# Attention kernel: row maxima moved inside the SBUF and turned once a pair, the scaling of the maxima on GpSimd, logarithms first among the loads

## The reference, cut to what matters

```python
log_G = cumsum(log_sigmoid(6.906768 + gate))
s = einsum('bthd,bshd->bhts', q, k) * scale
logits = 2 * log(abs(s) + 1e-30) + log_G[:, :, :, None] - log_G[:, :, None, :]
logits = where(tril, logits, -inf)
m = max(logits, axis=-1)
a = where(tril, exp(logits - m), 0)
y = einsum('bhts,bshd->bthd', a, v) / (sum(a, -1) + 1e-6)
y = (y - mean(y)) / sqrt(var(y) + 1e-9) * ln_w
```

## Time and profile before

| what | us |
|---|---|
| median of three runs | 2074.45 |
| the profiled execution's own time | 2080.6 |
| its span, first to last instruction | 2078.2 |
| TensorE busy in the span | 1939.0 |
| VectorE busy | 1765.1 |
| ScalarE busy | 1298.9 |
| GpSimd busy | 783.3 |

### The profile page before, as it was taken

The page is one execution under the profiler, slowest core; times in us unless marked ns, Lnnn a source line. Parts: engine busy times, 40 slices in busy tenths (PEclk is TensorE's granted clock), DMA queues, the critical chain, the costliest instruction groups (busy, mean ns, idle before and its releaser), DMA issues. The chain is left out here.

```text
span 2078.2 us, 37745 instructions
## 1 busy us (share of the span) xinstructions
PE 1939.0 (93%) x13187; PEld 1378.2 (66%) x13187; DVE 1765.1 (85%) x2747; ACT 1298.9 (62%) x2204; POOL 783.3 (38%) x687
## 2 busy tenths in 40 slices
PE   7999769999999999999999998799937999999997
PEld 5766525555555555555555554699837999999997
DVE  6999849999999999999999999677766878778774
ACT  5444457777777777777777775344425656656653
POOL 3777601121111112211211111366623665656553
PEclk9999979999999999999999999799966999999999
DMA  5888792455433455433555321444442433444343
GB/s 190 279 280 282 245 254 64 118 127 132 96 87 102 118 127 128 104 83 90 132 127 127 86 63 35 113 129 133 127 155 72 91 72 81 91 91 86 70 103 61
DMA packets 158247, 257.16 MB, mean 124 GB/s; under 512 B 48751, under 2 KB 122880, under 8 KB 151616
## 3 DMA queue, kind: packets, MB, share of 16 engines
q1 hardware_dynamic: 131824, 216.17, 37.3%
q0 software_dynamic: 15360, 20.99, 6.6%
q10 hardware_dynamic: 10896, 17.83, 2.6%
HBM read 159.19 MB, written 100.27 MB: 125 GB/s over the span
## 5 line engine op out<-in xcount | busy, mean ns | idle before, releaser
L999 ACT ACTIVATE att_sb_a<-att_ps_s,att_sb_fg,att_sb_f 128x1024 f32<-128x1024 f32 x384 | 454.1, 1201 | 230.0 <-PE att_ps_s L1144 218.9
L1037 DVE TENSOR_TENSOR keep_sb_store<-keep_sb_store,att_sb_a 128x1024 f32<-128x1024 f32 (+2 forms) x528 | 535.3, 1028 | 15.9 <-ACT att_sb_a L999 7.5
L955 POOL TENSOR_SCALAR_AFFINE_SELECT att_sb_dec<-att_sb_dec 128x128 f32<-128x128 f32 x256 | 178.4, 698 | 844.7 <-ACT att_sb_dec L989 844.7
L1163 PE MATMUL att_ps_off<-att_sb_a,att_sb_v 128*64 128x512 f32 x1520 | 365.5, 594 | 1.2 <-DVE att_sb_part L1064 1.1
L1855 ACT ACTIVATE ffn_sb_h<-ffn_ps_p,ffn_sb_b_cols 128x256 f32<-128x256 f32 x320 | 151.7, 476 | 179.8 <-PE ffn_ps_p L2038 152.7
L1144 PEld LDWEIGHTS att_ps_s<-att_sb_q,att_sb_k 64*128 64x128 f32 x1896 | 158.4, 185 | 115.7 <-issue 64.9
L1144 PE MATMUL att_ps_s<-att_sb_q,att_sb_k 64*128 64x512 f32 (+1 forms) x1896 | 229.0, 375 | 5.9 <-DMA att_sb_k<-k_rows 5.7
L1144 PEld LDWEIGHTS att_ps_s<-keep_sb_late,att_sb_k 64*128 64x128 f32 x1920 | 160.4, 185 | 110.2 <-issue 56.6
L1144 PE MATMUL att_ps_s<-keep_sb_late,att_sb_k 64*128 64x512 f32 (+3 forms) x1920 | 230.8, 374 | 0.3
L1954 DVE TENSOR_TENSOR ffn_sb_h_lo<-ffn_sb_h,ffn_sb_h_hi 128x256 fp32r<-128x256 f32 x320 | 200.6, 670 | 28.0 <-ACT ffn_sb_h_hi L1848 20.2
L1053 DVE SCALAR_TENSOR_TENSOR att_sb_a<-att_ps_s,att_sb_dec 128x1024 f32<-128x1024 f32 (+3 forms) x256 | 209.2, 817 | 7.7 <-PE att_ps_s L1144 5.3
(11 more groups left out here) (247 smaller groups left out, 3539.6 us busy)
## 6 DMA issues: line engine op xcount, KB each, us to landing
q_rows<-early_sb_halves SPq DMA_DIRECT2D x32, 1024.0 KB, 4.9
att_sb_k<-k_rows SPq DMA_DIRECT2D x60, 512.0 KB, 16.0
close_sb_nT<-num_rows SPq DMA_DIRECT2D x34, 512.0 KB, 4.0
k_rows<-early_sb_halves SPq DMA_DIRECT2D x16, 1024.0 KB, 5.1
keep_sb_late<-q_rows SPq DMA_DIRECT2D x32, 512.0 KB, 14.3
num_rows<-att_sb_num SPq DMA_DIRECT2D x64, 256.0 KB, 2.4
keep_sb_raw<-L_ffn_W ACTq DMA_DIRECT2D x32, 512.0 KB
att_sb_hb<-half_log SPq DMA_DIRECT2D x15, 1024.0 KB, 23.0
```

Of the source, the lines that this page charges most:

```text
L955: nc.gpsimd.affine_select(out=tile, in_=tile, compare_op=ALU.is_ge, fill=0.0, base=0, pattern=[[1, P]], channel_multiplier=-1).then_inc(de ...
L999: nc.scalar.activation(x, s_ps[slot(op)][:, :, :], ACT.Square, scale=f[:, p, i - 1, s:s + 1], bias=fg[:, p, i - 1, s:s + 1]).then_inc(sq_d ...
L1037: nc.vector.tensor_tensor(x[:, :, c:TB], x[:, :, c:TB], y[:, :, c:TB], ALU.max).then_inc(max_done, 1)
L1163: last = nc.tensor.matmul(ps[h * HD:(h + 1) * HD, c:TB], v_tile, a[:, a_slot(op), h, c:TB], start=(s == 0), stop=(s == (ST * i if kind == ...
```

## The change

It has four parts. (1) For pairs 0 to 14 the four max steps become one. SyncE moves the maxima of each block, once they are complete, inside the SBUF: a block's 128 partitions go in four DMAs of 32 partitions x 1024 numbers into four new tiles `tops`, so that block i takes partitions 32i to 32i+31 of each. VectorE folds the four tiles into one by three maxima (`fold`), TensorE transposes that one in eight transposes, and VectorE reduces it in two instructions (one a head, 128 x 512). The last pair keeps the old way. (2) `scale` goes from VectorE to GpSimd. (3) The logarithms are the first of a pair's loads; `factors` stands at 0.69 of a body. (4) `PATTERN` has 41 entries, with new offsets; SyncE and GpSimd get lists of their own in order of place. `keep.raw` is allocated after attention, since the new tiles need its place.

```diff
-PATTERN = ("d3 o1 o1 d3 o1 d3 d3 o1 o2 o2 o2 d1 o2 x0 x3 "
-           "o2 d1 o2 o2 d1 o2 d1 o3 d2 o3 o3 d2 d2 o3 o3 "
-           "d2 d0 o3 x1 o3 o3 o3 o3 d0 d0 x2 d0 o3 o3")
-CARRIED = ("d3", "x3", "x0")
+PATTERN = ("o1 d3 o1 d3 o1 d3 o1 d3 o2 o2 d1 o2 o2 d1 "
+           "o2 d1 o2 o2 d1 o2 o3 d2 o3 d2 o3 o3 d2 o3 "
+           "o3 d2 x0 o3 o3 d0 o3 d0 o3 o3 d0 o3 d0")
+CARRIED = ("d3", "x0")
+FOLDS = (0.50, 0.66, 0.68)
...
+    last = PAIRS - 1
+    for s, i in enumerate((1, 2, 0)):
+        place[last, "max", i, 0] = place[last, "diag", 3, s + 1] + 0.4
+    place[last, "max", 3, 0] = place[last, "diag", 3, ST - 1] + 8
...
-            return place[op] + 2.25 if op[3] else place[op[:3] + (1,)] + 2.24
-        return place[op] + 4.81
+            return place[op] + 3.32 if op[3] else place[op[:3] + (1,)] + 3.31
+        return place[op] + 5.7
...
-    dec_order = Order({op: place[op] - 5.95 for op in diags})
+    dec_order = Order({op: place[op] - 3.93 for op in diags})
...
-    own_order = Order({op: place[op] + 0.34 for op in diags})
+    own_order = Order({op: place[op] + 1.54 for op in diags})
...
+    folds = [(q, n) for q in range(PAIRS - 1) for n in range(1, ST)]
+    def fold_at(q, n):
+        return (q + 1 + FOLDS[n - 1]) * N
...
-    act_todo += [(q * N + N * 0.88, "factors", (q + 1,)) for q in range(PAIRS - 1)]
+    act_todo += [(q * N + N * 0.69, "factors", (q + 1,)) for q in range(PAIRS - 1)]
...
+    sp_todo = [(values_at(last_own(q, i)) + 1, "num", (q, i)) for q, i in owns]
+    sp_todo += [(max(max_at(last_own(q, i)), place[q - 1, "max", 0, 0] if q else 0) + 1, "top", (q, i))
+               for q, i in owns if q < PAIRS - 1]
+    sp_todo += [(values_at(last_own(q, 3)) + 2.5, "pair", (q + 2,)) for q in range(PAIRS - 2)]
+    pool_todo = [(place[op] - 3.93, "cut", op) for op in diags]
+    pool_todo += [(max_at(last_off(q, i)) + 0.01, "scale", (q, i)) for q, i in blocks]
...
             def load(q):
+                load_logs(q)
                 load_scored(...)
                 load_values(...)
-                load_logs(q)
...
+            def move(q, i):
+                sp.wait_ge(max_done, max_order.count(last_own(q, i)))
+                if q:
+                    sp.wait_ge(s_done, s_order.count((q - 1, "max", 0, 0)))
+                for n in range(ST):
+                    sp.dma_start(tops[n][i * FOLD:(i + 1) * FOLD, :],
+                                 acc[n * FOLD:(n + 1) * FOLD, i, :, :].rearrange("p h c -> p (h c)")).then_inc(moved[i], 16)
...
+            def scale(q, i):
+                x = acc[:, i, :, :]
+                pool.wait_ge(max_done, max_order.count(last_off(q, i)))
+                pool.wait_ge(et_done, et_order.count((q, i)))
+                nc.gpsimd.tensor_tensor(x, x, et[:, et_order.rank[q, i] % 2, None, :].to_broadcast([P, 2, TB]), ALU.mult).then_inc(scaled, 1)
...
+                if q and s == (0 if i == 0 else 1):
+                    dve.wait_ge(moved[i], 16 * ST * q)
...
+            def fold(q, n):
+                x, y = tops[0], tops[n]
+                if n == 1:
+                    for i in range(NB):
+                        dve.wait_ge(moved[i], 16 * ST * (q + 1))
+                else:
+                    dve.wait_ge(fold_done, 3 * q + n - 1)
+                nc.vector.tensor_tensor(x[:, :], x[:, :], y[:, :], ALU.max).then_inc(fold_done, 1)
...
+                for h in range(2):
+                    last = nc.vector.tensor_reduce(keep.row_max[:, q, :, h].rearrange("p (i c) -> p c i", c=ST),
+                                                   s_ps[slot(op)][:, h, :].rearrange("p (c i k) -> p c i k", c=ST, k=FOLD), AX.X, ALU.max)
...
+                    if q == PAIRS - 1:
+                        pe.wait_ge(max_done, max_order.count(last_own(q, i)))
+                    else:
+                        pe.wait_ge(fold_done, 3 * (q + 1))
+                        rows = tops[0]
```

More of the change, by code:

```diff
@@ L829, in attend @@
     av_order = Order({op: values_at(op) for op in offs + diags})
[L830 to L832 removed]
+    sq_order = Order({op: place[op] + (0 if op[1] == "off" else 2.34) for op in offs + diags})
+    dec_order = Order({op: place[op] - 3.93 for op in diags})
+    et_order = Order({(q, i): place[q, "off", i, 0] + 2.29 for q, i in blocks})
@@ L844, in attend @@
-    act_todo += [(place[q, "off", i, 0] - 1.18, "et", (q, i)) for q, i in blocks]
-    act_todo += [(q * N + N * 0.88, "factors", (q + 1,)) for q in range(PAIRS - 1)]
+    act_todo = [(place[op] + (0 if op[1] == "off" else 2.34), "sq", op) for op in offs + diags]
+    act_todo += [(place[op] - 3.93, "dec", op) for op in diags]
+    act_todo += [(place[q, "off", i, 0] + 2.29, "et", (q, i)) for q, i in blocks]
+    act_todo += [(q * N + N * 0.69, "factors", (q + 1,)) for q in range(PAIRS - 1)]
     dve_todo = [(max_at(op), "max", op) for op in offs + diags]
-    dve_todo += [(place[op] + 0.34, "own", op) for op in diags]
@@ L848, in attend @@
[L848 to L852, removed]
+    dve_todo += [(place[op] + 1.54, "own", op) for op in diags]
+    dve_todo += [(place[op] + 1.26, "row", op) for op in maxes]
@@ new lines, in attend @@
+    dve_todo += [(values_at(last_off(q, i)) + 1.17, "part", (q, i)) for q, i in blocks]
+    dve_todo += [(values_at(last_own(q, i)) + 0.42, "total", (q, i)) for q, i in owns]
+    dve_todo += [(fold_at(*op), "fold", op) for op in folds]
+    sp_todo = [(values_at(last_own(q, i)) + 1, "num", (q, i)) for q, i in owns]
+    sp_todo += [(max(max_at(last_own(q, i)), place[q - 1, "max", 0, 0] if q else 0) + 1, "top", (q, i))
+               for q, i in owns if q < PAIRS - 1]
+    sp_todo += [(values_at(last_own(q, 3)) + 2.5, "pair", (q + 2,)) for q in range(PAIRS - 2)]
@@ L895, in attend @@
         a = m.sbuf("a", [P, A, 2, TB])
+        tops = [m.sbuf(f"tops{i}", [P, 2 * TB]) for i in range(ST)]
         acc = store[:, :].rearrange("p (i h c) -> p i h c", i=NB, h=2)
@@ L902, in attend @@
         num_st = [m.sem(f"num_st{i}") for i in range(2)]
+        moved = [m.sem(f"moved{i}") for i in range(NB)]
+        fold_done = m.sem("fold")
         prep_done, et_done, exp_done, dec_done = (m.sem(s) for s in ("prep", "et", "exp", "dec"))
@@ L940, in _, with store_num @@
             load(1)
-            for n, (q, i) in enumerate(total_order):
+            def store_num(q, i):
+                n = total_order.rank[q, i]
                 sp.wait_ge(num_done, n + 1)
                 sp.dma_start(num_rows[q, :, i * TB:(i + 1) * TB], num[:, n % 2, :]).then_inc(num_st[n % 2], 16)
-                if i == 3 and q + 2 < PAIRS:
-                    load(q + 2)
+            def move(q, i):
[5 more added lines that the diff above has]
+                                 acc[n * FOLD:(n + 1) * FOLD, i, :, :].rearrange("p h c -> p (h c)")).then_inc(moved[i], 16)
+            for _, what, op in sp_todo:
+                if what == "num":
+                    store_num(*op)
+                elif what == "pair":
+                    load(*op)
+                else:
+                    move(*op)
             for i in range(2):
@@ L951, in _, with cut @@
             nc.clear_and_free_semaphores(used_up)
-            for n, (q, _, i, j) in enumerate(dec_order):
-                pool.wait_ge(exp_done, n + 1)
+            def cut(op):
+                _, _, i, j = op
+                pool.wait_ge(exp_done, dec_order.count(op))
                 tile = dec[:, OWNS.index(i) % 2, j, 0:P]
@@ L956, in _ @@
                                         pattern=[[1, P]], channel_multiplier=-1).then_inc(dec_done, 1)
+            def scale(q, i):
[3 more added lines that the diff above has]
+                nc.gpsimd.tensor_tensor(x, x, et[:, et_order.rank[q, i] % 2, None, :].to_broadcast([P, 2, TB]), ALU.mult).then_inc(scaled, 1)
+            for _, what, op in pool_todo:
+                if what == "cut":
+                    cut(op)
+                else:
+                    scale(*op)
         @block.scalar
@@ L1088, in _ @@
                     rows(op)
-                elif what == "scale":
-                    scale(*op)
+                elif what == "fold":
+                    fold(*op)
                 elif what == "part":
@@ L2181, in build @@
         keep.constants_in = m.sem("constants_in")
-        keep.raw = [m.sbuf(f"raw{i}", [P, KD * INNER // 2]) for i in range(2)]
         keep.raw_in = [m.sem(f"raw_in{i}") for i in range(2)]
@@ L2215, in build @@
             attend(nc, keep, early, first, used_up, store, late, q_rows, k_rows, v_cent, half_log, num_rows)
+        keep.raw = [m.sbuf(f"raw{i}", [P, KD * INNER // 2]) for i in range(2)]
         h2_rows = scratch("h2_rows", (NTT, P, D + TAG))
```

32 lines of the change are left out of this document (17 added, 15 removed).

## The result

The changed kernel took 2055.26 us (median of four, 2051.12 to 2056.08), against 2074.64 for the kernel before in the same comparison: a ratio of 0.990, 95% interval 0.9885 to 0.9919, or 19.4 us less. The forecast was 2033.5 with 2024 to 2060 around it: the direction and the range hold, the size is half of the forecast. It is the time that rival A gives (2055), though not quite by its mechanism.

What follows compares the result with a forecast made beforehand. TensorE's queue was taken to bound attention, VectorE 4% behind. Gains 45.9 + 1 less tail 2.3 and stalls 3.6 made 41.0 us off 2074.45, so 2033.5 us; range 2024 to 2060.

Steps and rivals of the forecast that it cites:

- rival A: Attention bodies: VectorE becomes the bound, a scale holding it 1.5 us; 61.3 us a body, 2055 us; chance 0.18.
- TensorE's gain: TensorE's queue: three max steps of 1.02 us go, 3.06 us a body, 45.9 us over 15 bodies.
- VectorE's own work: VectorE a body: 60.1 us, less 7.9 for scales and reduces, plus 4.6 for folds and half-size reduces, gives 56.8.
- GpSimd starts some 0.1 us after the maximum it waits for: Scale on GpSimd: starts 0.1 us after its maximum and holds till 2.4; two PSUM operations cover 1.65 of it.
- held time: VectorE's maxima held by the scales on GpSimd: 2.25 us a body, ends 0 and 7.0; VectorE then needs 59.05.
- stalls: TensorE and VectorE queues within 1%, coupled by score and `a` buffers: 0.25 us a body, 3.6 in all.
- The cut queued behind block 3's scale has 5.5 places ... cost nothing: GpSimd's queue: this cut has 5.5 places, 8 us, from its decay to its use, so cost nothing.
- One VectorE operation is let pass, not a run of them: GpSimd against VectorE: cuts get in after 1377 ns at the most, 292 of it their own.
- B: Attention bodies: slower by the GpSimd and VectorE lock; full 2.34 us held per scale, 63.8 a body, 2092 us; chance 0.07.
- C: SyncE's moves land late, 15 us and more; the first fold waits 7 us a body; 2135 us; chance 0.05.
- D: TensorE in attention: the change frees nothing, its time goes into waits for squares; 2074 us; chance 0.03.
- Logarithms: SyncE's loads: logarithms issued first land near 11.5 us, before `factors` 17.9 us after; cost 0, other end 5 us a body.

Runs made afterwards that it cites:

- the repetition: The changed kernel as it is, measured once more beside other runs on one chip: 2050.95 us, ratio 0.9886 to the kernel before.
- the scale ahead: Changed kernel with each scale one entry earlier in GpSimd's list, ahead of the cut that waits for a late decay: 2035.24 us, ratio 0.9801.

## Why the prediction was wrong, point by point

- **What bounds the kernel before, and TensorE's gain: right.** The need after is 59.36 us (run without the scale), 0.3 less than the 59.65 of the sum, since a max step is worth 1.14 us in its queue, not the 1.02 read from one pair of starts.
- **VectorE's own work: right.** Folds 1.23, reduces 0.68 us, 56.8 us a body without the scale; in the changed kernel busy 97.8% of 61.41 = 60.1 us, which is 56.8 plus 3.7 held within 0.4.
- **The step that failed: "GpSimd starts some 0.1 us after the maximum it waits for."** I walked VectorE's new queue from each scale on and never GpSimd's own. The two entries were there to be read, the cut 0.26 of a place ahead of the scale, and the cut waits for ScalarE, which runs behind its plan. So the scale began 1.86 us after its maximum in the mean, when the PSUM operations were partly or wholly over, and held a maximum for up to 2.2 us. Two edits that only start it in time gave 16 to 21 us back. In the terms of the sum: held time 3.7 us a body for 2.25, and stalls (the body over the larger of the two needs) 61.41 - 60.5 = 0.9 us (0.5 in the repetition) for 0.25. With the start as assumed, the walk was good: 1.9 us held against 2.25, 59.95 us a body against 59.9, 2035 against 2033.5. That last agreement is partly luck: the need was 0.3 lower and the stalls 0.6 instead of 0.25 us a body. (15 x 0.25 is 3.75, not the 3.6 of the sum; and the 109 GB/s of "The moves" is 103 in the earlier trace rows. Neither changes the forecast.)
- **The walk was of one body in three.** The matmuls with the values go in groups of three places (`GROUP`, L748), and 41 is no multiple of 3, so `before_own` and `total` fall before or behind a given maximum by body, and the order repeats every third. In the body I walked, block 1's scale is followed by a half-size maximum and two PSUM operations; in the one shown above by `before_own` alone. It moved the sum little (1.9 measured for 2.25), but it was not seen.
- **"The cut queued behind block 3's scale has 5.5 places ... cost nothing": right, and the wrong way round.** I asked what a scale does to the cuts behind it, not what a cut does to the scale behind it.
- **"One VectorE operation is let pass, not a run of them": wrong as a rule.** In the kernel before the longest cut was 1.38 us. In the changed kernel 31 of 256 last over 1.5 us and the longest 3.86. Here one starts at 611.08 and takes 3.85 us (the row holds it and the next, of 0.29): an operation of VectorE with two SBUF inputs is under way, and three more of them, back to back, go ahead of it. It cost little, since VectorE waited only 1.4 us in all for cuts. Why scales got in after one operation (they took 3.38 us at most, 2.38 their own) and this cut did not, is open.

```profile
611.08 4.09 POOL L993 TENSOR_SCALAR_AFFINE_SELECT att_sb_dec<-att_sb_dec 128x128 f32<-128x128 f32 x2 [4.23 <-ACT att_sb_dec L1039]
610.69 1.21 DVE L1089 TENSOR_TENSOR keep_sb_store<-keep_sb_store,att_sb_a 128x1024 f32<-128x1024 f32 x1
611.82 1.21 DVE L1129 TENSOR_TENSOR att_sb_tops<-att_sb_tops 128x1024 f32<-128x1024 f32 x1
612.96 1.81 DVE L1089 TENSOR_TENSOR keep_sb_store<-keep_sb_store,att_sb_a 128x512 f32<-128x512 f32 x2
```

- **Rival A** named the time (2055) and the amount held (1.5 us a scale against 3.7 / 3 = 1.2 measured), but its sign, VectorE at 99%, didn't come. VectorE at 99.6% runs at 59.95 us a body when nothing is held in a lump. By the rows, what a hold costs is the score buffer that isn't freed: TensorE's weight loads waited 56.8 us for `own_scores`, 4.1 before and 23.3 with the scale ahead.
- **B and the skill.** The Trainium skill, page "SBUF — State Buffer", section "Who interferes with whom", adds that issue order, not the operation's shape, decides who blocks. The scale that started at 718.35 held a maximum started at 718.43 for its whole length: there the trace agrees. It doesn't everywhere: the cut of 611.08, two points up, started ahead of three operations of VectorE and ran behind them. The loss was only that of the ones uncovered, so B's 2092 was far.
- **C (late moves) and D: right to leave.** Landing 2.4 us in the median, as in the nearest row taken, and under 5 us for block 3.
- **Logarithms: cost 0 was right; the other end, 5 us a body, was too small.** It is 8.2. **The tail** was right (1.0 against 1.3 in sum).

About 5 us of what is missing in the profiled execution is not held time but the clock, below; the repetition, which hasn't that, is at 60.98 us a body.

## What to carry to other kernels

An operation moved to an idle engine inherits that engine's queue: read what stands ahead of it there and what that waits for, before costing what it does to others. Where two engines exclude each other, the moment at which the operation starts is worth more than the engine's free time: here 16 to 21 us for one entry's place. And load is a poor guide to a stall: VectorE was harmless at 99.6% busy and dear at 97.8% with single operations of near 3 us in it.

## What was not expected of the hardware

- TensorE's clock fell in the middle of attention. Of the kernels shown, only the changed one and the one with the logarithms last, which stalls far longer, had this. TensorE in order of time, in one of the three bodies of the changed kernel where it did, then the clock (the third number from the end) of two windows of 5 us:

```profile
747.64 0.55 PE L1211 MATMUL att_ps_s<-keep_sb_late,att_sb_k 64*128 64x128 f32 x6 [0.65 <-DVE att_sb_a L1099]
748.87 1.77 PE L1190 MATMUL att_ps_s<-keep_sb_ident,att_sb_tops 128*128 128x128 f32 x8 [0.67 <-DVE att_sb_tops L1129]
```

```profile
563.00:568.00 5.00, 4.19 (x20) 2.40 (x22) 5.00 (x7) 3.34 (x11) 1.00 (x1) 0.67 0.92 200
748.00:753.00 5.00, 4.33 (x20) 2.36 (x20) 5.00 (x7) 2.85 (x11) 0.99 (x1) 0.66 0.88 210
```

TensorE had waited twice for 0.65 and 0.67 us, and the granted clock in the 5 us that hold the restart was 0.66 in the mean, that is, part of the time at 1.2 GHz and the rest at 2.4; the kernel with the scale ahead has 1.00 there. The falls are 184 us apart, three bodies, as the order of the queue repeats. Half speed for the missing part costs 5 x 0.34 = 1.7 us each time, 5 us for three. The repetition shows what the waits do not decide. It has the same two waits at the same place, and the clock stays at 1.00:

```profile
744.97 0.55 PE L1211 MATMUL att_ps_s<-keep_sb_late,att_sb_k 64*128 64x128 f32 x6 [0.65 <-DVE att_sb_a L1099]
746.20 1.06 PE L1190 MATMUL att_ps_s<-keep_sb_ident,att_sb_tops 128*128 128x128 f32 x8 [0.67 <-DVE att_sb_tops L1129]
745.00:750.00 5.00, 4.33 (x28) 2.30 (x30) 5.00 (x6) 3.20 (x11) 0.98 (x1) 1.00 0.87 199
```

The eight transposes take 1.06 us there and 1.77 in the fall. So these waits go with a fall in one execution and with none in another; what else decides is open. Nor do the falls explain the 4.3 us between the two medians: two of the slower executions, 2055.84 and 2054.68 us, have the same mean clock, 0.964, as the fast one of 2051.12.

- The same load of 1 MB lands after 9.8 us in the median as the first of ten issued together (4.9 to 17.2, the changed kernel), and after 24.0 as the last (22.8 to 34.1, the kernel with the logarithms last): here the order of issue is worth 14 us.
- Each of the two kernels with the divided scale had one execution of several milliseconds (6477 and 3141 us) among six, which the other kernels didn't show. It stays open, and I would not take that version before it is known why.
